# Input projection of the next image made block by block inside the scan, and an interleaved gate and output stage

## What is computed

```python
# layer 0: group norm, then a gated selective scan
x = x + L0(group_norm(x))
#   xz = in_proj_w @ x          (192 -> 768 channels)
#   xx, z = split(xz)           (384 and 384)
#   u = gelu(depthwise 3x3 conv(xx) + b)
#   4 directions k, 16 states n:  h = h * exp(delta * A) + delta * u * B ;  y += h * C
#   y = layer_norm(y) * ln_w + ln_b
#   out = out_proj_w @ (y * gelu(z))
# layer 1: group norm, then attention over the 2304 positions, 4 heads of 48
x = x + L1(group_norm(x))
#   qkv = depthwise 3x3 conv(w_qkv @ x + b), q and k normed, softmax(q k^T t) v, w_proj
```

## Time and profile before

| | |
|---|---|
| median of 3 runs | 15768.13 us (15763.9 to 15773.21) |
| the profiled execution | 15775.06 us, span 15772.2 us from first to last instruction |
| granted TensorE clock, mean | 0.962 |
| busy | PE 84%, DVE 82%, ACT 70%, POOL 67% of the span |
| DMA | 1278 MB, mean 81 GB/s |

### The profile page before, as it was taken

One profiled execution on the slowest core, in us unless ns is written; L12 is line 12 of the kernel. 1 busy time (PEld: TensorE's weight loads), 2 busy tenths in 40 slices (PEclk: granted clock), 3 DMA queues, 4 the chain that ended last, 5 costly groups with the idle time before them and its releaser, 6 DMA issues.

```text
span 15772.2 us, 244463 instructions
## 1 busy us (share of the span) xinstructions
PE 13228.5 (84%) x60812; PEld 7904.7 (50%) x60812; DVE 12892.5 (82%) x13792; ACT 11049.2 (70%) x22630; POOL 10577.1 (67%) x4228
## 2 busy tenths in 40 slices
PE   6888888888888898888988879888898888988889
PEld 4555455554555545555455544555445554455544
DVE  8998579985799848998489984899849998399983
ACT  5886578765787657886578855787557885578855
POOL 6997069970799607996079950899508994099940
PEclk8999999999999999999999999999999999999999
DMA  2332023320233203332033320333203331033310
GB/s 90 116 113 87 5 86 115 115 83 5 90 117 114 78 5 95 116 114 74 5 101 114 116 67 5 106 114 115 63 5 110 116 113 58 5 115 116 116 52 10
DMA packets 822802, 1278.12 MB, mean 81 GB/s; under 512 B 27617, under 2 KB 815201, under 8 KB 816289
## 3 DMA queue, kind: packets, MB, share of 16 engines
q1 hardware_dynamic: 821600, 1264.99, 25.5%
HBM read 1241.29 MB, written 23.59 MB: 80 GB/s over the span
## 4 chain that ended last, share of the span: by engine, by line
PE 37%; issue 21%; DVE 20%; ACT 9%; POOL 8%; DMA 2%; ACTq 1%; DVEq 1%; SPq 0%; POOLq 0%
DVE area L920 14%; PE ps L751 8%; PE ps L762 8%; POOL area L1385 7%; PE ps L572 6%; DVE area L938 4%; ACT ps L1177 3%; ACT area L1157 2%; PE ps L559 2%; DMA area<-bc_rows 2%; PE ps L538 1%; PE ps L480 1%; POOL area L1395 1%; PE ps L502 1%; PE ps L648 1%
## 5 line engine op out<-in xcount | busy, mean ns | idle before, releaser
L920 DVE TENSOR_TENSOR_SCAN area<-ps,hst,area 128x384 f32<-128x384 f32 x9216 | 8591.7, 993 | 222.0 <-ACT ps L1177 212.1
L1385 POOL TENSOR_TENSOR area<-area 128x1152 f32<-128x1152 f32 x3072 | 7998.8, 2638 | 46.3 <-DVE area L920 28.2
L1177 ACT ACTIVATE ps<-area,a_neg 128x384 f32<-128x384 f32 x9216 | 5334.3, 582 | 1706.5 <-DVE area L920 1524.7
L572 PE MATMUL ps<-area,ident 128*128 128x384 f32 x12672 | 4731.3, 507 | 203.5 <-ACT area L1163 111.0
L572 PEld LDWEIGHTS ps<-area,ident 128*128 128x128 f32 x12672 | 2319.9, 196 | 1922.3 <-ACT area L1163 403.0
L559 PE MATMUL ps<-ident,area 128*128 128x128 f32 x17280 | 2465.9, 280 | 6.0 <-ACT area L1157 6.0
L550 PE MATMUL ps<-ident,area 128*128 128x128 f32 x8640 | 1506.1, 284 | 1024.1 <-ACT area L1157 971.6
L559 PEld LDWEIGHTS ps<-ident,area 128*128 128x128 f32 x17280 | 2233.8, 196 | 64.5 <-ACT area L1157 10.9
L1319 ACT ACTIVATE area<-ps,t_neg,area 128x768 f32<-128x768 f32 x1728 | 1617.8, 986 | 908.3 <-PE ps L751 908.3
L1395 POOL TENSOR_TENSOR area<-area 128x1152 f32<-128x1152 f32 x768 | 2026.8, 2639 | 135.2 <-ACT hst L1135 134.2
L550 PEld LDWEIGHTS ps<-ident,area 128*128 128x128 f32 x8640 | 1041.4, 142 | 2040.0 <-ACT area L1157 1471.2
(11 more groups left out here) (124 smaller groups left out, 9595.9 us busy)
## 6 DMA issues: line engine op xcount, KB each, us to landing
area<-bc_rows SPq DMA_DIRECT2D x1536, 768.0 KB, 6.4
area<-in_x SPq DMA_DIRECT2D x17, 1728.0 KB, 10.0
out<-area SPq DMA_DIRECT2D x8, 1728.0 KB, 8.4
bc_rows<-area SPq DMA_DIRECT2D x8, 576.0 KB, 4.6
bc_rows<-area SPq DMA_DIRECT2D x8, 480.0 KB, 4.1
w_dt<-in_w_dt SPq DMA_DIRECT2D x1, 768.0 KB, 6.4
bc_rows<-area SPq DMA_DIRECT2D x8, 96.0 KB, 2.1
w_in<-in_w_in SPq DMA_DIRECT2D x1, 576.0 KB, 4.8
```

The source lines that it names most:

```text
L572: m = e.matmul(ps[:, 5 + j, 0:CH], ident[:], hb[:, i % NH, j], start=i == 0, stop=i == N - 1)
L920: e.tensor_tensor_scan(rev(hb[:, i % NH, j], k), rev(ps[:, 2 + j, 0:CH], k), rev(dbu[:, i % NH, j], k), hst[:, i, j:j + 1], ALU.mult, ALU. ...
L1177: e.activation(ps[:, 2 + j, 0:CH], dlt[:, par, j], ACT.Exp, scale=a_neg[:, j, k, i:i + 1]).then_inc(da, 1)
L1385: e.tensor_tensor(dbu[:, i % NH], du[:, par], row_b[:, q % 2, i % ROWS:i % ROWS + 1].broadcast_to([128, J, CH]), ALU.mult).then_inc(dbus, 1)
```

## The change

The first image's projections are made up front. For every later image, in directions k = 0, 1, 2 (UK = 3) of the scan of the image before it, each of the 18 blocks makes two units: one 128-channel by 384-position piece of xx (on PE after slot m = 10) and one of z (after slot m = 14). The unit reads a piece of the normed image that SP loads (`xz`), lands in PSUM bank 1, is copied by ACT to a staging tile, and SP stores that to device memory (`x_padded`, `z_raw`). z (3.4 MB) is loaded back in the first block of k = 3, xx tile by tile into two padded tiles during the attention. The projection in the attention, the weight staging on POOL and the z projection in `back` are gone. `w_qkv` and `w_pr` are loaded anew for each image into memory that the scan used.

```diff
+UK = 3
+UC = UK * NC
+UNIT_AT = (10, 14)
...
 SP
+            def store_x(b, k, c):
+                e.wait_ge(unit_ev, b * 2 * UC + c * 2 + (2 * NC * k + 1))
+                alone(e)
+                ... e.dma_start(dst[:, ...], x_st[...]).then_inc(xi_out, 16)
+            def store_z(b, k, c):
+                e.wait_ge(unit_ev, b * 2 * UC + c * 2 + (2 * NC * k + 2))
+                alone(e)
+                e.dma_start(z_d[...][:, ds(c * CH, CH)], z_st[:]).then_inc(z_out, 16)
+            def load_x(b, k, c):
+                e.wait_ge(unit_mm, b * 2 * UC + c * 2 + (2 * NC * k + 2))
+                alone(e)
+                e.dma_start(xz[:], xn_d[...][:, :, ds(c * CH, CH)]).then_inc(xz_in, 16)
                 for q in range(4):
+                        if q == 0 and last and last[0] < UK:
+                            store_z(b, *last)
+                        if q == 3 and k < UK:
+                            store_x(b, k, c)
+                        if q == 1 and k == UK and last[0] < UK:
+                            ...
+                            e.dma_start(z_v, z_d[...]).then_inc(z_in, 16)
                         if q < 3:
                             b_group(g, k, c, q + 1)
                         ...
                         c_group(g, k, c, q)
+                        if q == 0 and k < UK:
+                            load_x(b, k, c)
 PE, scan
+                def unit(k, h, gd, i):
+                    e.wait_ge(hcs, gd + (1 + DVE_N.index((8, 12)[i]) + 1))
+                    e.wait_ge(xz_in, h * 16 + 16)
+                    for t in range(CT):
+                        at = i * DI + k * 128
+                        m = e.matmul(ps[:, 1, 0:CH], w_in[:, t, at:at + 128], xz[:, t], start=t == 0, stop=t == CT - 1)
+                    m.then_inc(unit_mm, 1)
                         slot(g, m)
+                        if k < UK and m in UNIT_AT:
+                            unit(k, h, gd, UNIT_AT.index(m))
 ACT, scan
+                def unit_out(h, i):
+                    e.wait_ge(unit_mm, h * 2 + (2 + i + 1))
+                    e.wait_ge(xi_out if i == 0 else z_out, h * 16 + 16)
+                    ... e.activation(x_st or z_st, ps[:, 1, 0:CH], ACT.Copy).then_inc(unit_ev, 1)
                             e.activation(ps[:, 2 + j, 0:CH], dlt[:, par, j], ACT.Exp, ...
+                            if k < UK and j == 0 and i - 1 in UNIT_AT:
+                                unit_out(h, UNIT_AT.index(i - 1))
 PE, back (the loops over all blocks for L626, L637 and L648 go)
+                for c in range(NC):
+                    variance(c)
+                    if c >= 2:
+                        out_proj(c - 2)
+                out_proj(NC - 2)
+                out_proj(NC - 1)
 DVE, back (gated: three L959 and three L968; residual: two L978 and two L981)
+                gated(0)
+                gated(1)
+                e.wait_ge(x_in, b * 32 + 48)
+                for c in range(NC):
+                    if c + 2 < NC:
+                        gated(c + 2)
+                    residual(c)
 ACT, back
+                e.preload_act_table_set("gelu_and_others")
+                e.wait_ge(z_in, b * 16 + 16)
+                for j in range(J):
+                    e.activation(z_v[:, j], z_v[:, j], ACT.Gelu).then_inc(z_ge, 1)
+                e.preload_act_table_set("natural_log_exp_and_others")
 PE, attention
-                        if p == 1:
-                            e.wait_ge(ex, base + 3)
-                            in_proj_tile(b * 3 + c + 3)
 ACT, attention
-                        if p == 1:
-                            e.wait_ge(conv, b * 54 + c * 18 + 54)
-                            pad_tile(b * 3 + c + 3)
 SP, image (between the scan and the store of the result)
+                e.dma_start(w_qkv, t["w_qkv"]).then_inc(w_at, 16)
+                e.dma_start(w_pr, t["w_pr"]).then_inc(w_at, 16)
                 wait_cv2(e, b, QT - 1)
                 e.dma_start(xf, t["x"][ds(nxt, 1)]...).then_inc(x_in, 16)
+                e.wait_ge(gn_v, b * 2 * GN_OPS + 4 * GN_OPS)
+                e.dma_start(xn_d[ds(b + 2, 1)]..., xf).then_inc(xn_out, 16)
+                e.wait_ge(xi_out, b * 16 * UC + 16 * UC + 16)
+                e.wait_ge(n_mm, b * 14 + 14)
+                for j in range(J):
+                    if j == 2:
+                        e.wait_ge(conv, b * 54 + (54 + 18))
+                    e.dma_start(xpad_l[j % 2], xi_d[ds(b + 1, 1), j:j + 1]...).then_inc(xi_in[j % 2], 16)
```

More of the change, by code:

```diff
@@ L629, in back @@
[L629 to L650, removed]
+                def variance(c):
+                    e.wait_ge(sqs, b * 6 + (c + 1))
+                    e.wait_ge(nrm, b * 18 + (3 * c + 3))
+                    for j in range(J):
+                        m = e.matmul(ps[:, c % 2, 0:CH], mean_m[:], sq_v[:, j, c * CH:(c + 1) * CH],
+                                     start=j == 0, stop=j == J - 1)
+                    m.then_inc(var_mm, 1)
@@ new lines, in out_proj @@
+                def out_proj(c):
+                    e.wait_ge(gate, b * 18 + (3 * c + 3))
+                    for h in range(CT):
+                        e.wait_ge(x1s, b * 12 + (2 * c + h + 1))
+                        for j in range(J):
+                            m = e.matmul(ps[0:CP, 2 + 2 * (c % 2) + h, 0:CH], w_out[:, j, h * CP:(h + 1) * CP],
+                                         y_v[:, j, c * CH:(c + 1) * CH], start=j == 0, stop=j == J - 1)
+                        m.then_inc(o_mm, 1)
@@ L888, in c_columns @@
                         m.then_inc(ct_cp, 1)
+                e.wait_ge(xn_out, b * 16 + 16)
+                alone(e)
                 by_columns(0)
@@ L961, in back @@
-                e.wait_ge(nrm, b * 18 + 24)
-                alone(e)
-                with e.Fori(0, 3) as cc:
-                    for s in range(2):
-                        for j in range(J):
-                            o = y_v[:, j, ds(cc * 2 * CH + s * CH, CH)]
-                            e.wait_ge(z_ge, b * 18 + cc * 6 + (3 * s + j + 7))
-                            e.scalar_tensor_tensor(out=o, in0=o, scalar=ln_b[:, j:j + 1],
-                                                   in1=z_v[:, j, ds(cc * 2 * CH + s * CH, CH)],
-                                                   op0=ALU.add, op1=ALU.mult).then_inc(gate, 1)
@@ new lines, in residual @@
+                def residual(c):
+                    for h in range(CT):
+                        xo = x_v[:, h, c * CH:(c + 1) * CH]
+                        e.wait_ge(o_mm, b * 12 + (2 * c + h + 1))
+                        e.tensor_tensor(xo, xo, ps[0:CP, 2 + 2 * (c % 2) + h, 0:CH], ALU.add).then_inc(x1s, 1)
+                    for h in range(CT):
+                        e.wait_ge(x1s, b * 12 + (2 * c + h + 5))
+                        e.bn_stats(gst[:, h, c], x_v[:, h, c * CH:(c + 1) * CH]).then_inc(gn_v, 1)
@@ L1082, in _, with softplus @@
             for j in range(J):
-                if j:
-                    wait_conv(e, 0, j - 1)
+                if j == 2:
+                    wait_conv(e, 0, 0)
                 pad_tile(j)
-            def softplus(g, par, k, op, j, bank=1):
+            for j in range(J):
+                for c in range(NC):
+                    e.wait_ge(z_mm, 6 * j + c + 1)
+                    e.activation(z_first[:, j, c * CH:(c + 1) * CH], ps[:, c, 0:CH], ACT.Copy).then_inc(z_ge, 1)
+            group_std(1, 0)
+            def softplus(g, par, k, op, j, bank=1, h=None):
                 x, y = dlt[:, par, j], du[:, par, j]
@@ L1142, in c_copy @@
                         e.wait_ge(dp_rd, g * 3 + (3 + 1))
+                    if h is not None and i == 14:
+                        e.wait_ge(unit_ev, h * 2 + 2)
                     if nxt and i in (5, 8, 11):
```

273 lines of the change are left out of this document (154 added, 119 removed).

## The result

| | before | after |
|---|---|---|
| median | 15766.01 us (15762.36 to 15773.21, 4 runs) | 16007.48 us (16004.96 to 16018.07, 3 runs) |
| profiled execution, span | 15775.06, 15772.2 | 16004.96, 16003.1 |
| granted clock, mean | 0.962 | 0.957 |

The ratio is 1.0154, 95% interval 1.0134 to 1.0174: 241 us slower. The forecast was 15,825, 57 us slower, in a range of 15,650 to 16,030. The sign and the range hold; the size is nearest to rival (c), 16,070.

A forecast was written before the change was run, and what follows sets the result against it. DVE, with POOL also full, was taken to bound the scan and PE the stretches outside. Added to the median 15768: -190 - 208 + 331 + 72 + 32 + 20 = +57, so 15,825 us, range 15,650 to 16,030.

The forecast's parts named there:

- rival (c): Scan: SP's row loads late in every block, landings near 9.1, z in ring order; +302, 16,070 us; chance 0.23.
- attention: Attention: PE no longer runs input projection tiles that hold back the scores; gain 23.7 us per image, 190 in eight.
- `back`: Stage `back`: z's projection goes, PE interleaves variances and output projections; gain 26.0 us per image, 208 in eight.
- unit stalls: Scan: ACT's copy of each unit delays the exp DVE needs, 1.15 us twice a block in 144 blocks; +331.
- SP's queue: Scan: `store_x` waits for ACT's copy, so C rows of states 12 to 15 go out later; 0.5 us a block, +72.
- z loaded back: First block of k = 3: z's 3.4 MB load may delay the next rows; 4 us per image, +32.
- start: Before the first front: first image's z, its store, loading image 1, statistics and a norm; +20, bounds 10 and 30.
- the early GELU of `back`: Stage `back`: ACT does GELU first, its squares begin some 4 us later; costs nothing, as they wait for DVE's centring anyway.
- The two gaps: Scan, blocks with k < 3: DVE idles about 1.15 us at the second channel tile of states 11 and 15.
- Rival (b): Scan: new stalls take the place of DVE's old idle time, 166 not paid again; -213, 15,555 us; chance 0.08.
- Rival (a): Scan: the waits on ACT alone decide, SP's row loads are in time; -47, 15,721 us; chance 0.22.
- my 5.9 us of lateness: First block of k = 3: C rows behind z's load in ring order land 5.9 us late, 47 in eight images.

The follow-up runs named there:

- late copies: The changed kernel with ACT copying a unit out of PSUM after the third exp of state 11 or 15, not the first: 16139.05 us, ratio 1.0233.

## Why the prediction was right, and by how much it was off

The runs give every term a size. Units, with rows in time: 15654.81 - 15363.12 = 292. SP's order: 16007.48 - 15654.81 = 353. The rest: 15363.12 - 15766.01 = -403.

| term | forecast | measured |
|---|---|---|
| attention | -190 | 25.2 per image, -202 |
| `back` | -208 | 26.6 per image, -212 |
| unit stalls | +331 | +292 |
| SP's queue | +72 | +353 |
| z loaded back | +32 | about 0 |
| start | +20 | +14 |

- **Right:** attention and `back` in mechanism and size. The second table load and the early GELU of `back` showed no cost. The two gaps stand where they were placed, 1.08 and 1.04 us against 1.15, once rows are in time.
- **Mis-sized: "SP's queue", 0.5 us a block taken, 2.5 measured.** Its upper bound, 302, was passed too. Three things were missing. First, I timed the issue from an x copy that itself came on time (4.3 us later; it was 5.2), and gave the C rows 6.4 us to land, the middle of B and C rows together; the C rows of states 12 to 15 alone took 7.1 before the change, the B rows 5.5 (my count). Second, I counted the late C row once, at DVE's product, and not again behind it: ACT's in-order queue, PE's in-order turn, the z unit. DVE's own gap at that product is 81 us in all, 0.56 a block, so the 0.5 was right for the first payment, and only for it. Third, the sentence "the pair behind `store_z` has B rows with 5 us to spare" costed one load of that pair. The other brings the C rows of states 0 to 3, which landed 6.3 us after the block's first scan, not 0.7 before it, and POOL waited 409.6 us for rows. Moving `store_z` alone gained 97. The test that I wrote down, a C copy's wait of 1.5 us a block for rival (c), came out at 433.9 / 144 = 3.0: (c) it was.
- **Rival (c)** named the place, but its reasons were late landings and z in ring order. Landings of C rows did grow, by 0.5 us for states 12 to 15 and by 1.6 and 1.8 for states 0 to 3 and 4 to 7 (my count); the larger part was the issue, 5.2 us later in the block.
- **z loaded back.** The SP issues of the load and of the next row pair in image 1, DVE's first scan of the block, and then the landing times of that pair (minimum, median, maximum) and of the load:

```profile
3215.87 0.38 SPq L483 DMA_DIRECT2D area<-z_raw  x1
3220.47 1.01 SPq L415 DMA_DIRECT2D area<-bc_rows  x2
```

```profile
3216.88 2.83 DVE L1018 TENSOR_TENSOR_SCAN area<-ps,hst,area 128x384 f32<-128x384 f32 x3
```

```profile
DMA to landing us min/median/max: 13.7/14.4/15.1
```

```profile
DMA to landing us min/median/max: 16.2/16.2/16.2
```

  The load landed at 3232.1, the rows behind it at 3234.2 and 3236.2, in the order of issue; without such a load they need 5.5 us (B rows) and 6.8 (C rows of states 4 to 7, my count). That agrees with the rule of the Trainium skill's page "DMA: Bandwidth & Descriptors", Queues, rings and completion order, that each DMA engine consumes one issuer's descriptors in ring order; my 5.9 us of lateness did not follow. I had put the end of z's data 21.5 us after the first scan. It was 15.2, so the C rows came at 19.3, ahead of the 21.6 at which they are wanted. Mean blocks of k = 3 did not change.
- **Rival (b)** was partly true beside the others: the old gaps shrank by 90 us. **Rival (a)** is what the stores behind the rows give: 15654.81, against 15,721 forecast for it; the stalls were 39 us cheaper, and the rest (-403 where -378 was in its sum) 25 better.
- **My expectation for the late copies** failed by the same blind spot: it followed ACT and DVE, not what SP holds back behind a copy.

- **Luck.** With SP's term at 353 and the others as forecast, the sum is 16,106, outside the range. The other terms came out 93 us lower in all (39 of it the stalls, 32 z), and only that keeps the time inside.

Still open: how the 353 us divide between the late issue and the crowding of two pairs 4.2 us apart, and whether the 22 us by which the gains of the two stores overlap are more than the spread of the runs.

## What to carry to other kernels

A store that waits for a compute engine must not stand ahead of loads that the same engines need: put it behind them, where the wait holds nothing. Cost every load behind a new wait, not the first of a pair only, and follow a late operand down each in-order queue until it meets slack, since it is paid again wherever another queue waits in order. Moving work later on one engine pays only after what it releases has been moved out of the way: the same edit lost 132 us alone and gained 292 with it.

## What was not expected of the hardware

- How long the load of a 288 KB piece takes to land went by how close behind a pair of rows it was issued. In the changed kernel it is 0.8 us behind (my count) and takes 8.6 us; with both stores behind their rows it is 7.1 us behind and takes 3.5; with the units left out it is 0.8 us behind again and takes 7.6, though that pair is in time:

```profile
xz<-x_normed SPq DMA_DIRECT2D x144, 288.0 KB, 8.6
```

```profile
xz<-x_normed SPq DMA_DIRECT2D x144, 288.0 KB, 3.5
```

```profile
xz<-x_normed SPq DMA_DIRECT2D x144, 288.0 KB, 7.6
```

- Rows issued 4.2 us behind another pair landed after 8.6 us (C rows of states 4 to 7), and after 6.9 where 12.3 us lay between the pairs.
- 187 MB more of DMA (1278 to 1466 MB) cost no measurable time by themselves: without the units the kernel took 15380.76 us.
